# First stage of a transformer block: a sine product kept in PSUM, normalising split over two engines, loops written out, two loads moved

## The chip, the cores and the metric

One Trainium2 chip, one of its cores. The metric is the time of one execution on the device in microseconds. Engines: TensorE (PE; its weight loads are PEld), VectorE (DVE), ScalarE (ACT), GpSimd (POOL) and SyncE (SP), which only issues DMAs here. All times below are microseconds unless marked ns.

## The reference, cut to what matters

Four sequences of 1024 rows with 128 features, float32. The change is in the first part: normalise the rows, project them to queries, keys and a 32-wide latent, rotate, and apply gelu.

```python
def _layernorm(x, axis=-1, eps=1e-05):
    m = jnp.mean(x, axis=axis, keepdims=True)
    v = jnp.var(x, axis=axis, keepdims=True)
    return (x - m) / jnp.sqrt(v + eps)

def _apply_rope(x, cos, sin):
    x1, x2 = (x[..., :d // 2], x[..., d // 2:])
    return x * cos + jnp.concatenate([-x2, x1], axis=-1) * sin

# attention on xn = _layernorm(x); 16 heads of 8; E - DR = 0, so q and k are the rotated parts alone
q_r = _apply_rope(x @ wqr + bqr, cos, sin)
k_r = _apply_rope(x @ wkr + bkr, cos, sin)
ckv = _gelu(x @ wkv + bkv)
v = (ckv @ wv + bv).reshape(b, s, H, HD).transpose(0, 2, 1, 3)
q, k = _gelu(q_r), _gelu(k_r)            # split in heads
attn = softmax(causal(q k^T / sqrt(8)))  # then attn @ v, @ wo + bo, layernorm, residual
```

Behind it come a mixture of eight experts with a shared one and a last normalisation. They are as before.

## The kernel before

The kernel has one first stage, closed by a barrier of all engines, and then a long part in which attention, routing and experts overlap. The first stage cuts the 4096 rows into 8 chunks of 512 (`CHUNKS`), two to a sequence; `pair(j)` handles chunks 2j and 2j + 1, and p is the parity of a chunk. The four pairs run through `peeled`: pair 0 and pair 3 are written out, pairs 1 and 2 are a loop on each engine, with waits and addresses worked out in registers.

For chunk c the engines do this, each in its own order:

- ScalarE issues the load of x for chunk c + 2 (L501), makes the latent `ckvT` (L504), rounds the second bfloat16 part of chunk c - 1 (`part_mid`, L493, twice), copies the turned rows of chunk c + 1 from PSUM (`keep_xT`, L485), waits until the stores of chunk c - 2 have landed, and applies gelu to q and then to k, each twice: `full` in float32 (L515) and `parts` in bfloat16 (L516). Between the two it copies v (L519).
- VectorE makes four products, projection plus bias times cosine or sine (L558): q with cosine, q with sine, k with cosine, k with sine. The cosine product goes to `direct`, the sine product to `turned`, both in SBUF; a sum of both (L562) follows each sine product. After the q half come the statistics of chunk c + 2 (L325, L329, and the variance step L332), after the k half the normalising of chunk c + 2 in four tiles (L536).
- TensorE multiplies for the latent (L596), q with plain and swapped columns, then turns the normalised rows of chunk c + 1 (L583, four transposes), then k with plain and swapped columns (L599), then v (L605). The four products for VectorE lie in banks 1 to 4 of PSUM.
- GpSimd computes the inverse root for chunk c + 2 (L443), the remainder `rest` after the first bfloat16 part (L448) and the third part (`part_low`, L453), for q and for k. Its order is k's rest and both low parts of chunk c - 1, the root, then q's rest of chunk c.
- SyncE stores v and six parts of q and k of chunk c - 1 to DRAM (`store`, L396 and L400). Before the stores of chunk 5 it issues `load_group` for group 0 and before those of chunk 6 for group 1. A group is four heads of one sequence, ten DMAs (L285 to L295). Groups 0 and 1 belong to sequence 0, so chunks 0 and 1 are all that they need.

After chunk 7 TensorE waits for all products and for group 0, and computes scores for 18 items (L305); VectorE takes their row maxima (L316). The barrier follows when SyncE has seen all stores land (L421).

What orders work around the change: `pe.wait_ge(xn_ok, c + 1)` ahead of the turn; `wait(act, stored[p], ...)` ahead of the gelus of chunk c, for chunk c - 2; `wait(dve, gelu_ok, 4 * c - 4)` ahead of the products of chunk c, as `direct` has two buffers; and in PE `wait(pe, rope, ...)`, by which a bank is overwritten only after VectorE's product has read it.

## Time and profile before

| | us |
|---|---|
| median of 3 runs | 838.52 (838.01 to 841.66) |
| profiled execution | 839.22 |
| its span | 837.5 |
| TensorE busy | 753.9 (90%) |
| VectorE busy | 620.7 (74%) |
| ScalarE busy | 510.1 (61%) |
| GpSimd busy | 338.3 (40%) |
| first stage, to the barrier | 96 |

Busy is time in which an engine worked on the program's instructions, summed over the whole span; it hides that stages have different limits. For the change one reads the first 96 us alone: the busy time per stretch, and then the order of instructions on each engine with the idle time in front of each and what ended it ("<-"). A trailing q (SPq, ACTq) marks what an engine's sequencer does, here the issue of DMAs.

### The profile page before, as it was taken

How to read it: one execution, taken by the hardware profiler on the slowest of the kernel's cores; microseconds unless marked ns; L12 is line 12 of the kernel's file. 1: busy time of each engine (PE TensorE's matmuls, PEld its weight loads, DVE VectorE, ACT ScalarE, POOL GpSimd, SP SyncE). 2: the span in 40 equal slices, each digit the busy share in tenths (PEclk: the TensorE clock that was granted, in tenths of full speed). 3: DMA queues.
4: the chain of work that ended last, by engine and by line, in shares of the span. 5: the costliest groups of instructions: out<-in, count | busy, mean ns of one | idle time of the engine just before them, and what ended most of it. 6: DMA issues, size and time to landing. Idle time of an engine off the chain costs nothing.

```text
span 837.5 us, 17519 instructions
## 1 busy us (share of the span) xinstructions
PE 753.9 (90%) x5660; PEld 361.6 (43%) x5660; DVE 620.7 (74%) x1942; ACT 510.1 (61%) x1047; POOL 338.3 (40%) x517
## 2 busy tenths in 40 slices
PE   5876689999999999999999999999989889898994
PEld 2332133333334334334333433433336768786861
DVE  5998878988887896886897887888445566465636
ACT  2664046666766877766778666687887534343525
POOL 3775121222221331234543215453257276464624
PEclk9997579999999999999999999999999999999998
DMA  6459462431632423405324224141312325232153
GB/s 161 149 156 178 119 166 31 67 52 17 116 57 44 79 46 73 80 8 110 59 61 94 53 39 86 40 98 40 118 37 71 104 79 146 72 85 71 50 205 112
DMA packets 78187, 71.84 MB, mean 86 GB/s; under 512 B 26939, under 2 KB 58076, under 8 KB 77916
## 3 DMA queue, kind: packets, MB, share of 16 engines
q1 hardware_dynamic: 69472, 59.87, 32.4%
q0 software_dynamic: 4352, 8.99, 3.4%
q10 hardware_dynamic: 4274, 1.87, 0.9%
q8 instruction: 47, 0.77, 0.4%
q14 instruction: 42, 0.34, 0.1%
HBM read 44.27 MB, written 23.94 MB: 81 GB/s over the span
## 4 chain that ended last, share of the span: by engine, by line
PE 62%; DVE 11%; issue 7%; ACT 6%; POOL 1%; DMA 1%; POOLq 0%; SPq 0%; DVEq 0%; ACTq 0%
PE ps L2171 14%; PE ps L2198 14%; PE ps L305 11%; DVE x_in L316 5%; PE ps L1668 4%; ACT expT L1895 4%; PE ps L1649 2%; PE ps L1651 2%; PE ps L1657 2%; PE ps L1650 2%; PE ps L1573 1%; PE ps L2148 1%; PE ps L1586 1%; ACT rows L747 1%; PE ps L972 1%
## 5 line engine op out<-in xcount | busy, mean ns | idle before, releaser
L1895 ACT ACTIVATE expT<-ps 128x512 f32<-128x512 f32 (+1 forms) x640 | 333.0, 554 | 149.6 <-PE ps L2198 143.4
L316 DVE CUSTOM_DVE_ANT_0 x_in<-ps,mask 128x1024 bf16<-128x1024 f32 (+7 forms) x512 | 364.3, 754 | 60.5 <-PE ps L305 57.0
L2198 PE MATMUL ps<-q_space,k_space 96*128 96x512 bf16 (+3 forms) x768 | 223.6, 334 | 8.8 <-ACT expT L1895 5.1
L305 PE MATMUL ps<-k_space,q_space 96*128 96x512 bf16 (+3 forms) x768 | 197.6, 343 | 22.1 <-DVE mx L316 15.5
L2171 PE MATMUL ps<-expT,vr 128*9 128x256 f32 (+1 forms) x2560 | 178.3, 360 | 0.9 <-POOL expT L1849 0.9
L1849 POOL TENSOR_SCALAR_AFFINE_SELECT expT<-expT 128x512 f32<-128x512 f32 x128 | 79.7, 634 | 195.9 <-ACT expT L1895 195.5
L2198 PEld LDWEIGHTS ps<-q_space,k_space 96*128 96x128 bf16 x768 | 62.1, 98 | 160.3 <-ACT expT L1895 103.1
L305 PEld LDWEIGHTS ps<-k_space,q_space 96*128 96x128 bf16 x768 | 64.1, 100 | 86.2 <-DVE mx L316 49.0
L1255 POOL DMA_INDIRECT expert_rows<-expT,tile_to x72 | 69.2, 961 | 49.8 <-ACT expT L1326 24.1
L737 POOL DMA_INDIRECT sorted_rows<-rows,places x64 | 64.2, 1003 | 58.2 <-ACT expT L1895 33.9
L2171 PEld LDWEIGHTS ps<-expT,vr 128*9 128x9 f32 x2560 | 41.3, 88 | 92.2 <-issue 47.1
L1318 ACT ACTIVATE q_space<-ps 128x512 f32<-128x512 f32 x36 | 21.5, 597 | 56.4 <-PE ps L1651 56.4
L1802 POOL TENSOR_SCALAR negs<-mx 128x16 bf16<-128x16 f32 x32 | 8.4, 263 | 108.6 <-DVE mx L316 96.6
L1496 DVE TENSOR_TENSOR q_space<-q_space,ps 128x512 f32<-128x512 f32 x36 | 24.7, 687 | 35.3 <-ACT q_space L1318 35.3
L1668 PE MATMUL ps<-w_gu,k_space 128*128 x288 | 41.4, 287 | 2.5 <-DVE k_space L1503 2.4
L316 DVE DVE_READ_ACCUMULATOR2_ANT mx<- 128x1 f32 x512 | 42.5, 83 | 0.0
L1649 PE MATMUL ps<-w_hi,rows_hi 128*128 x72 | 35.4, 492 | 4.3 <-issue 2.8
L1668 PEld LDWEIGHTS ps<-w_gu,k_space 128*128 128x128 f32 x288 | 34.9, 191 | 9.8 <-issue 9.7
L1503 DVE COPY k_space<-ps 128x512 f32<-128x512 f32 x36 | 24.9, 692 | 15.5 <-PE ps L1657 15.3
L1326 ACT ACTIVATE expT<-ps,expT 128x128 f32<-128x128 f32 x72 | 22.5, 365 | 17.8 <-PE ps L1668 17.8
L1651 PE MATMUL ps<-w_hi,rows_lo 128*128 x72 | 29.5, 410 | 0.0
L1650 PE MATMUL ps<-w_lo,rows_hi 128*128 x72 | 29.4, 408 | 0.0
(228 smaller groups left out, 934.1 us busy)
## 6 DMA issues: line engine op xcount, KB each, us to landing
q_space<-q_parts SPq DMA_DIRECT2D x48, 192.0 KB
expT<-sorted_rows SPq DMA_DIRECT2D x72, 65.0 KB, 2.1
k_space<-k_parts SPq DMA_DIRECT2D x32, 128.0 KB
expT<-expert_rows SPq DMA_DIRECT2D x16, 256.0 KB, 5.4
q_parts<-parts SPq DMA_DIRECT2D x24, 128.0 KB, 2.4
k_parts<-parts SPq DMA_DIRECT2D x24, 128.0 KB, 3.2
k_space<-k_parts SPq DMA_DIRECT2D x16, 192.0 KB
v_ones<-v_st SPq DMA_DIRECT2D x8, 288.0 KB, 3.2
```

The source lines that it names most:

```text
L305: last = nc.tensor.matmul(psw[:, at + lo:at + hi], qr[:, g % RING, hh, qi * P:(qi + 1) * P], kr[:, g % RING, hh, lo:hi], start=True, stop= ...
L316: last = nc.vector.tensor_tensor_reduce(out=unread[:, odd, col:col + width], in0=psw[:, 2 * CT * odd + col:2 * CT * odd + col + width], in ...
L737: nc.gpsimd.indirect_dma_start(out=xs_d, out_offset=bass.IndirectOffsetOnAxis(ap=pos[:, q, k, c * NT + t:c * NT + t + 1], axis=0), in_=xs[ ...
L1255: nc.gpsimd.indirect_dma_start(out=y_d, out_offset=bass.IndirectOffsetOnAxis(ap=to[:, r, i:i + 1], axis=0), in_=yt[:, r, i], in_offset=Non ...
L1649: nc.tensor.matmul(out, hi, wide_hi[:, bass.ds(at, 2 * INTER)], start=True, stop=False)
L1650: nc.tensor.matmul(out, hi, wide_lo[:, bass.ds(at, 2 * INTER)], start=False, stop=False)
L1651: nc.tensor.matmul(out, lo, wide_hi[:, bass.ds(at, 2 * INTER)], start=False, stop=True).then_inc(gu_ok, 1)
L1668: last = nc.tensor.matmul(out, hT[:, q % 2, INTER * i + P * f:INTER * i + P * (f + 1)], wide_down[:, bass.ds(at + P * f, P)], start=f == 0 ...
L1849: nc.gpsimd.affine_select(out=tile, in_=tile, compare_op=ALU.is_ge, fill=0.0, base=0, pattern=[[0, GH], [1, P]], channel_multiplier=-1).th ...
L1895: act.activation(expT[:, (NS * g + s) % PTN, hh, 0:width], ps[:, B_S + hh % 2, 0:width], ACT.Exp, scale=SCALE).then_inc(exp_ok, 1)
L2171: last = nc.tensor.matmul(ps[32 * hh:32 * hh + VW, B_O + half, at:at + n], vr[:, g % RING, kt, hh * VW:(hh + 1) * VW], expT[:, (NS * g + s ...
L2198: last = nc.tensor.matmul(ps[:, B_S + hh % 2, col:col + m], kr[:, g % RING, hh, kt * P:(kt + 1) * P], qr[:, g % RING, hh, q0:q0 + m], star ...
```

## The change

It is in the first stage only. Five things change:

- The sine product is written back to the PSUM bank from which it was read, and the sum reads it there. `turned` is gone. TensorE's next product into that bank waits for the sum (`added`) instead of the product (`rope`).
- Of the four tiles of a chunk VectorE normalises two; ScalarE normalises the other two, with scale `rstd1` and bias `nb1`, a new 128 x 4 product of minus mean and inverse root that VectorE makes first. ScalarE does this at the end of its chunk, for chunk c + 2, and in the prologue for chunks 0 and 1.
- The turn on TensorE and the root on GpSimd wait for ScalarE's half too.
- The loops over pairs are written out on all engines; waits and addresses are constants.
- `load_group` for group 0 comes ahead of the stores of chunk 3 and for group 1 ahead of those of chunk 5.

```diff
@@ helpers: peeled, at_row and wait_apart are removed @@
-def peeled(eng, n, body):
-
-    body(0)
-    with eng.Fori(1, n - 1) as i:
-        body(i)
-    body(n - 1)
@@ ln_stats @@
-            wait_apart(dve, steps, base + 1, passed_dve)
+            dve.wait_ge(steps, base + 1)
@@ first stage, tiles and semaphores @@
-            turned = sb(one, "turned", [P, 2, CT])
+            nb1 = sb(one, "nb1", [P, 2, NT])
...
+            xn_act = sem(one, "xn_act")
+            nb_ok = sem(one, "nb_ok")
+            BY_DVE = NT // 2
...
+            GROUP0_AT = 4
@@ sync @@
-                    qb, kb, vb = at_row(qd, j), at_row(kd, j), at_row(vd, j)
+                    qb, kb, vb = qd[j], kd[j], vd[j]
...
-                        if not exists(j + 1, PAIRS):
-
-                            if p == 0:
-                                sp.wait_ge(rows_in, DMA * 2 * RING)
-                                for i in range(2):
-                                    sp.wait_ge(stored[i], DMA * NSTORE)
-                            load_group(sp, p)
-                        if isinstance(j, int) and j == 0:
+                        if 2 * j + p == GROUP0_AT:
+                            sp.wait_ge(rows_in, DMA * 2 * RING)
+                            for i in range(2):
+                                sp.wait_ge(stored[i], DMA * NSTORE)
+                        if 2 * j + p in (GROUP0_AT, GROUP0_AT + 2):
+                            load_group(sp, (2 * j + p - GROUP0_AT) // 2)
+                        if j == 0:
...
-                peeled(sp, PAIRS, pair)
+                for j in range(PAIRS):
+                    pair(j)
@@ gpsimd @@
                 def root(c, p):
                     pool.wait_ge(ln, 3 * c + 3)
                     wait(pool, xn_ok, c - 1)
+                    wait(pool, xn_act, c - 1)
@@ scalar @@
+                def normalize_act(c, p):
+                    act.wait_ge(nb_ok, c + 1)
+                    for t in range(BY_DVE, NT):
+                        last = act.activation(x1[:, p, t], x1[:, p, t], ACT.Identity, scale=rstd1[:, p, t:t + 1],
+                                              bias=nb1[:, p, t:t + 1])
+                    last.then_inc(xn_act, 1)
+
+                normalize_act(0, 0)
                 keep_xT(0, 0)
+                normalize_act(1, 1)
                 act.wait_ge(w_in, DMA * W_DMAS)
...
-                            act.dma_start(x1[:, p], at_row(x_v, j + 1)[p]).then_inc(x_ok[p], DMA)
+                            act.dma_start(x1[:, p], x_v[j + 1, p]).then_inc(x_ok[p], DMA)
...
+                        if exists(c + 2, CHUNKS):
+                            normalize_act(c + 2, p)
@@ vector @@
                 def normalize(c, p):
                     dve.wait_ge(rstd_ok, c + 1)
-                    for t in range(NT):
+                    nc.vector.scalar_tensor_tensor(nb1[:, p], mv1[:, p, :, 0], -1.0, rstd1[:, p], ALU.mult,
+                                                   ALU.mult).then_inc(nb_ok, 1)
+                    for t in range(BY_DVE):
...
-                            dst, table = ((direct[:, p, i // 2], cos), (turned[:, i // 2], sin))[i % 2]
-                            if i % 2:
-                                wait(dve, added, 2 * c + i // 2 - 1)
+                            dst, table = ((direct[:, p, i // 2], cos), (ps[:, 1 + i], sin))[i % 2]
...
                                 nc.vector.tensor_tensor(direct[:, p, i // 2], direct[:, p, i // 2],
-                                                        turned[:, i // 2], ALU.add).then_inc(added, 1)
+                                                        ps[:, 1 + i], ALU.add).then_inc(added, 1)
@@ tensor @@
                 def turn(c, p):
                     pe.wait_ge(xn_ok, c + 1)
+                    pe.wait_ge(xn_act, c + 1)
...
                         for i, w in enumerate((w_q, w_qs, w_k, w_ks)):
-                            wait(pe, rope, 4 * (c - 1) + 1 + i)
+                            if i % 2:
+                                wait(pe, added, 2 * (c - 1) + i // 2 + 1)
+                            else:
+                                wait(pe, rope, 4 * (c - 1) + 1 + i)
...
-                pe.wait_ge(rope, 4 * CHUNKS)
+                pe.wait_ge(added, 2 * CHUNKS)
```

## Rows read from the trace of the kernel before

**Rows 1.** The page's head: the span of the profiled execution.

```profile
span 837.5 us, 17519 instructions
```

**Rows 2.** Busy time of each engine by stretch; then granted clock, DMA share, GB/s.

```profile
16.00:58.00 42.00, 34.92 (x125) 15.95 (x124) 39.23 (x106) 26.16 (x47) 29.50 (x25) 1.00 0.51 154
...
76.00:96.00 20.00, 13.83 (x36) 2.66 (x35) 17.06 (x48) 3.82 (x7) 4.53 (x4) 0.50 0.85 192
```

**Rows 3.** Timeline (start, duration, engine, line, tiles), end of the stage; SyncE's wait there.

```profile
91.51 0.60 SPq L400 DMA_DIRECT2D k_parts<-parts  x1
95.76 0.08 DVE L316 DVE_READ_ACCUMULATOR2_ANT mx<- 128x1 f32 x1
96.13 1.28 ACT L1895 ACT_TABLE_LOAD   x1 [13.28 <-PEq L334]
...
SPq L421 <- DMA k_parts<-parts: 2.7, 1, 2.7
```

**Rows 4.** Timeline of VectorE: one chunk, and the variance step of another.

```profile
34.18 0.74 DVE L558 SCALAR_TENSOR_TENSOR direct<-ps,cols,cos 128x512 f32<-128x512 f32 x1
...
35.62 1.50 DVE L562 TENSOR_TENSOR direct<-direct,turned 128x512 f32<-128x512 f32 x1
37.03 1.10 DVE L536 TENSOR_SCALAR x_in<-x_in,mv,rstd 128x128 f32<-128x128 f32 x4
...
40.74 0.87 DVE L325 BATCH_NORM_STATS2 st<-x_in 128x6 f32<-128x128 f32 x4 [0.56 <-DMA x_in<-in_x]
...
42.28 0.75 DVE L558 SCALAR_TENSOR_TENSOR direct<-ps,cols,cos 128x512 f32<-128x512 f32 x1
...
57.80 0.72 DVE L332 TENSOR_SCALAR ve<-mv 128x4 f32<-128x4 f32 x1
```

**Rows 5.** Timeline of GpSimd: one rest, and two low parts.

```profile
35.41 1.15 POOL L448 TENSOR_TENSOR rest<-full,parts 128x512 f32<-128x512 f32 x1
...
55.75 2.74 POOL L453 TENSOR_TENSOR parts<-rest,parts 128x512 bf16<-128x512 f32 x2
```

**Rows 6.** Timeline of ScalarE behind the k sum of one chunk.

```profile
37.14 0.63 ACT L515 ACTIVATE full<-direct 128x512 f32<-128x512 f32 x1 [2.25 <-DVE direct L562]
...
38.77 0.61 ACT L493 ACTIVATE parts<-rest 128x512 bf16<-128x512 f32 x1
```

**Rows 7.** Operations like the new ones, elsewhere: ns min/median/max; for ScalarE busy, mean ns.

```profile
L1496 DVE TENSOR_TENSOR q_space<-q_space,ps x36: 686/686/689, 675.4 to 794.3; 128x512 f32<-128x512 f32 x36
...
L1907 DVE MEMSET ps<- x1: 912/912/912, 96.4 to 96.4; 128x1024 f32 x1
...
L1370 DVE SCALAR_TENSOR_TENSOR out_shift<-out_mean_var,out_rstd x8: 146/146/164, 813.8 to 830.7; 128x4 f32<-128x4 f32 x8
...
L747 ACT ACTIVATE attn_rows<-attn_rows,shift,rstd 128x128 f32<-128x128 f32 x28 | 13.7, 495 | 0.2 <-DVE shift L823 0.2
```

**Rows 8.** The load of x: an issue in the timeline, and us to landing of all six.

```profile
37.61 0.39 ACTq L501 DMA_DIRECT2D x_in<-in_x  x1
...
DMA to landing us min/median/max: 2.8/3.0/4.5
```

**Rows 9.** Timeline: group 0's first DMA; ScalarE's q gelu of chunks 5 and 7.

```profile
62.88 0.36 SPq L285 DMA_DIRECT2D q_space<-q_parts  x1
...
57.55 0.63 ACT L515 ACTIVATE full<-direct 128x512 f32<-128x512 f32 x1 [0.61 <-DMA k_parts<-parts]
...
78.28 0.63 ACT L515 ACTIVATE full<-direct 128x512 f32<-128x512 f32 x1 [6.82 <-DMA k_parts<-parts]
```

**Rows 10.** Timeline of TensorE: turn of chunk 7, its last product, the first scores.

```profile
62.36 0.66 PE L583 MATMUL ps<-identf,x_in 128*128 128x128 f32 x4 [1.64 <-DVE x_in L536]
...
69.41 1.02 PE L599 MATMUL ps<-xnT,w_ks 128*128 128x512 f32 x2
...
75.93 1.55 PE L305 MATMUL ps<-k_space,q_space 96*128 96x512 bf16 x4 [4.41 <-DMA q_space<-in_const]
```

**Rows 11.** TensorE by stretch: length, busy (instructions), granted clock, DMA share, GB/s.

```profile
70.63:74.05 3.42, 0.89 (x8) 1.00 1.04 155
...
671.38:674.79 3.41, 3.01 (x9) 0.50 0.24 86
```

## What the change is predicted to do, and why

> **What bounds the kernel now.** I read the windows by stage first, then the end of the first stage, then one chunk of it engine by engine. The execution took 839.22 us, 1.7 over its span of 837.5 [rows 1]; the median of the three timed runs is 838.52, 0.7 below it. The change touches only the first stage, which ends at a barrier: VectorE ends its 18th maximum at 95.84, SyncE sees its last store landed at 91.51 + 0.60 + 2.7 = 94.8, and the next stage starts at 96.1 [rows 3]. So two paths end together there, 1.0 us apart. In the steady part VectorE is busy 39.23 of 42.00 us, GpSimd 29.50, and the DMA engines have a mean share of 0.51 [rows 2].
>
> One chunk of 512 rows takes 8.1 us, from its third product at 34.18 to the next one's at 42.28 [rows 4]. VectorE inside it: the k sum at 35.62 which takes 1.50, four normalisings of 1.10, and later a wait of 0.56 for x before the statistics [rows 4]. The 1.50 is a hold: GpSimd's rest runs 35.41 to 36.56, and the sum ends 0.55 after it; against a PSUM operand the same shape takes 0.69 and always does (686/686/689) [rows 4, 5, 7]. The variance step shows the same hold: at 57.80 it takes 0.72 and ends at 58.52, just behind GpSimd's two low parts, 55.75 to 58.49 [rows 4, 5]. So a second path of about the same length runs k sum, ScalarE, GpSimd's low parts, variance step.
>
> **Part by part.** Let s be the start of the third product of a chunk (34.18).
> - *Sine product in PSUM.* The k sum ends at s + 1.44 + 0.69 = s + 2.13, not s + 2.94. The write into PSUM is not in the trace for this operation. The nearest row, a memset of 1024 columns into PSUM, took 0.91, 0.46 for 512 [rows 7], so the write doesn't limit a product of 0.74; I take 0.74. The bounds are 0.60 and 0.90, 0.3 us a chunk either way.
> - *The hold moves on.* The new shift (0.15 by its twin in the last stage, [rows 7]) has two SBUF inputs, and it now arrives at s + 2.1 while GpSimd's rest still runs, to s + 2.38 [rows 5]. So the shift waits 0.3 and ends at s + 2.5; two normalisings of 0.26 pitch end at s + 3.0. Before it was s + 3.87. VectorE gains 0.85 a chunk. Unheld it would be 1.1, held by the whole rest again 0.5.
>   The Trainium skill (SBUF — State Buffer, section Who interferes with whom) says that an instruction with at most one SBUF input doesn't contend with GpSimd, and that two SBUF inputs or a two-port tensor_scalar do. By its rule the sum is freed, but the shift and the normalising behind it stay exposed, which speaks against part of the gain: 0.85, where the freed sum and two normalisings less would give 1.1. The trace agrees [rows 4, 5, 7].
> - *Half the normalising on ScalarE.* Two of 0.49, with an overlap of 0.06 each, are 0.86 [rows 7]. They stand behind both gelus of the k half and ahead of everything else of ScalarE. The queue behind the k sum runs full, parts, ckvT in 1.63 (37.14 to 38.77), then mid in 0.61 [rows 6]; GpSimd's first low part needs that mid. It now starts at the sum + 1.66 + 0.86 + 0.61 + 0.16 = sum + 3.3. The low parts took 2.74, with a hold by VectorE's q sum in it; two like the rest of 1.15 are 2.3 [rows 5], and the q sum's operand is in PSUM now, so I take 2.3. They end at s + 2.13 + 3.3 + 2.3 = s + 7.7, and hold the variance step until then. So the chunk falls from 8.1 to 7.7, not to the 7.15 that VectorE alone would take. TensorE's turn of the next rows waits for ScalarE's half, at the sum + 2.0, not only for VectorE's. Over the three chunks before the load that is 0.4 each, less 0.5 that I allow for the prologue, where ScalarE still issues the weights' DMAs and loads a table: 0.7 in all. TensorE's products wait for the sum instead of the product in alternate banks; these are done 3 us ahead, cost 0.
> - *Loops written out.* The x load of the next chunk but one was issued at 37.61, 0.49 after the k sum, and lands after 3.0 (2.8/3.0/4.5) [rows 4, 8]. It now stands behind the shift's wait, at s + 2.6, lands at s + 5.6 and is wanted at s + 5.1. This 0.5 is inside the 7.7. The bounds are 0 and, if ScalarE issued it only when its second normalising starts, 1.0 later: a chunk of 8.0.
> - *Rows of groups 0 and 1.* SyncE issued group 0's ten DMAs from 62.88, ahead of the stores of chunk 5. They filled the ring: those stores landed for ScalarE at 78.28, 15.4 us after the load's start, and ScalarE stood still for 6.82; without a load it waits 0.61 in the same place [rows 9]. Now the load stands ahead of the stores of chunk 3. It starts two chunks of 8.1 earlier, at 46.7 in the old time, 45.4 in the new (0.7 by the shorter chunks, 0.6 of loop work on SyncE between its issues). So chunk 3's stores land at 45.4 + 15.4 = 60.8, and 1.0 later with one load of x beside them. I take 61.8; the bounds are 58 (the DMA engines idle half the time) and 64. ScalarE needs them for the first gelu of chunk 5, which it was ready for at 57.55 - 0.61 = 56.9 and would now be at 55.6. It stands still for 6.2.
>   Queued behind this wait on ScalarE are that gelu, parts, v and the two k gelus, 0.54 each (three in 1.63), and then its half of normalising chunk 7: 5 x 0.54 + 0.86 = 3.6. So TensorE's turn of chunk 7 comes at 61.8 + 3.6 = 65.4. Before, it came at 62.36 [rows 10], after VectorE alone. TensorE is in order: the k products of chunk 6, v, and all of chunk 7 stand behind the turn, 8.1 us to the end of the last product (62.36 to 70.43) [rows 10]. TensorE would be through at 73.5. But it will have been idle some 5 us, from about 60. After it ran 0.89 us in the 3.42 before 74.05 its granted clock was 0.50, the lower level [rows 11]; so I expect the lower level when it resumes, and full clock back after dense work, as at 671.38 to 674.8 [rows 11]. That costs half of the dense time at the lower level, some 5.3 us: 2.7. TensorE is through at 76.2, VectorE's last product and sum end 1.5 later, at 77.7.
>   Before, VectorE ended at 74.0, but the scores started at 75.93, when group 0 had landed after a wait of 4.41 [rows 10]. So this wait of 1.9 goes and the scores start 1.8 later, at 77.7.
> - *18 maxima.* 19.9 us from scores to the end at the lower clock. I take 0.4 off, for the first 3.4 us at full clock; the bounds are 0 and 2 (full clock throughout). The stage ends at 77.7 + 19.9 - 0.4 = 97.2, 1.4 later than 95.84.
> - *Stores.* Group 1's load stands where group 0's stood, so chunk 5's stores land near 78 again and ScalarE goes on as before to 84.4. The stores of chunk 7 no longer stand behind a second load: they end near 91.5, not 94.8. This path no longer sets the end.
>
> The sum: 839.22 + 1.4 = 840.6; 0.7 less for the median is 839.9. I round to **839.7 us**.
>
> **The rivals.**
> 1. *The load is hidden* (faster). In the steady part the DMA engines have half their time free [rows 2]. If the ring drains by 56, ScalarE never stands still, TensorE's turn comes 1.3 before the old 62.36, at 61.1 (the sum 2.2 earlier by five shorter chunks and its own 0.8, ScalarE's half 0.9 later than VectorE's four were), its end at 69.2, VectorE's at 70.7; the maxima end at 90.2. Then the stores decide, at 89 (group 1's load 2 us earlier) to 91.5. The stage is 4.3 to 5.8 shorter: 833 to 834. For it: the free half. Against: the 15.4 us are from the same pattern of issues, load and then stores, on the same ring. Chance 0.22.
> 2. *TensorE stays at the lower clock* (slower). Place: the 8.1 us behind the turn of chunk 7. If the clock doesn't come back during it, it takes 16.2 in place of 10.8; end of stage 102.6, total 845. It decides if the clock is still at 0.50 when chunk 7's first product runs. For it: between 76 and 96 TensorE worked 13.83 of 20 us and stayed at 0.50 [rows 2]. Against: the recovery at 674.8 [rows 11]. Chance 0.10.
> 3. *ScalarE issues x late.* Chunks of 8.0, so load and stall come 1 us later, 841. The trace shows x issued at 37.61 behind a gelu of 37.14 and its twin, so with one activation in front of it not yet started, and no deeper case [rows 6, 8]. Chance 0.10. The Trainium skill (Advanced Engine Details and Errata, section Engine Queue Depths) gives ScalarE a queue of 8; by it x would be issued as soon as the shift is made, and this rival would not occur.
> 4. *The normalising doesn't go cheaply to ScalarE.* If Identity and Gelu needed different tables, two table loads of 1.28 [rows 3] would come in each chunk: 10.3 in place of 8.1, over six chunks 13 more, 852. Between exponentials it needed none (28 of 495 ns) [rows 7]. Chance 0.03.
>
> **How the numbers follow.** The forecast has 0.55, and its own range, from a load landing at 58 to 64 with the clock kept or lost, is 836.5 to 843. A difference of 0.5% (4.2 us) is about what a measurement of this kernel tells from none. Faster by more: 0.20, most of rival 1. Slower by more: 0.15, rivals 2 and 4 and the forecast's upper tail. Within: 0.65. The range for 8 in 10 takes in rival 1 and leaves out rivals 2 and 4 and a little more: 833.0 to 844.0.
>
> **What would show it.** The sum with PSUM at 0.69 in every chunk; the shift held to 0.4; chunks of 7.7; ScalarE's first gelu of chunk 5 idle for 4 to 7 us on a store; TensorE idle before the turn of chunk 7, with the clock at 0.50 behind it; scores within 0.3 of VectorE's last sum; the stage's end at 95 to 98. If ScalarE doesn't stand still there, rival 1 holds and the stage ends near 91.

## Result, and the profile after

| | before | after |
|---|---|---|
| median, us (5 runs each) | 838.52 (837.08 to 841.66) | 845.19 (843.81 to 848.76) |
| ratio to before | | 1.0077, 95% interval 1.0043 to 1.0111 |
| profiled execution, us; its span | 839.22; 837.5 | 848.76; 847.0 |
| end of the first stage (table load of the next one) | 96.13 | 105.90 |
| third product of chunks 0, 1, 2 and 5 | 18.21, 26.20, 34.18, 58.44 | 23.69, 31.14, 39.05, 66.53 |

The kernel became slower by 6.7 us, under 1%, where 1.2 was forecast. In the profiled execution the whole loss lies in the first stage: its end comes 9.8 us later, the span is 9.5 longer. That execution is the longest of its five, 3.6 above their median; a long stretch at TensorE's lower clock, shown below, has about that size.

The first stretch of it, timelines of SyncE, ScalarE's queue and VectorE in the changed kernel (start, duration, engine, line, operation, tiles; in brackets how long the engine stood still, and what released it):

```profile
9.63 0.38 SPq L268 DMA_DIRECT2D k_space<-in_const  x1
...
11.39 0.30 SPq L268 DMA_DIRECT2D q_space<-in_const  x1
...
11.83 0.40 ACTq L489 DMA_DIRECT2D x_in<-in_x  x1
...
22.29 0.87 DVE L298 BATCH_NORM_STATS2 st<-x_in 128x6 f32<-128x128 f32 x4 [5.53 <-DMA x_in<-in_x]
...
23.69 0.74 DVE L549 SCALAR_TENSOR_TENSOR direct<-ps,cols,cos 128x512 f32<-128x512 f32 x1
```

The rows of chunk 2 are asked for at 11.83. ScalarE's order now has its half of normalising chunk 1 ahead of this load, and that half waits for VectorE's shift; so the load also comes behind all six constant fills of SyncE. VectorE has chunk 2's rows at 22.29, after 10.5 us. Before the change the same load was issued beside the first fill, and VectorE found the rows in place (timelines of the kernel before):

```profile
9.74 0.42 ACTq L501 DMA_DIRECT2D x_in<-in_x  x1
...
16.82 0.86 DVE L325 BATCH_NORM_STATS2 st<-x_in 128x6 f32<-128x128 f32 x4
```

Chunk 0's third product is 5.5 us late. Only the shorter chunks eat into that: 4.9 at chunk 2, 3.6 at chunk 4 (53.97 for 50.38).

One undisturbed chunk, VectorE, GpSimd and ScalarE's queue, to compare with [rows 4 to 6]:

```profile
46.51 0.74 DVE L549 SCALAR_TENSOR_TENSOR direct<-ps,cols,cos 128x512 f32<-128x512 f32 x1
47.17 0.74 DVE L549 SCALAR_TENSOR_TENSOR ps<-ps,cols,sin 128x512 f32<-128x512 f32 x1
47.95 0.69 DVE L553 TENSOR_TENSOR direct<-direct,ps 128x512 f32<-128x512 f32 x1
48.55 0.27 DVE L526 SCALAR_TENSOR_TENSOR nb<-mv,rstd 128x4 f32<-128x4 f32 x1
...
52.02 0.87 DVE L298 BATCH_NORM_STATS2 st<-x_in 128x6 f32<-128x128 f32 x4 [0.63 <-DMA x_in<-in_x]
...
53.34 0.71 DVE L305 TENSOR_SCALAR ve<-mv 128x4 f32<-128x4 f32 x1
53.97 0.74 DVE L549 SCALAR_TENSOR_TENSOR direct<-ps,cols,cos 128x512 f32<-128x512 f32 x1
...
51.76 2.27 POOL L431 TENSOR_TENSOR parts<-rest,parts 128x512 bf16<-128x512 f32 x2 [0.70 <-ACT parts L481]
...
48.87 0.37 ACTq L489 DMA_DIRECT2D x_in<-in_x  x1
```

The sum takes 0.69, the write into PSUM costs nothing (0.74), the shift 0.27. The low parts start at 51.76, held by ScalarE's mid copy, and end at 54.03; the variance step, 0.71 where 0.17 is its own time, ends with them. The chunk takes 7.46, from 46.51 to 53.97.

Around the load of group 0, SyncE, ScalarE, VectorE and TensorE:

```profile
50.47 0.49 SPq L258 DMA_DIRECT2D q_space<-q_parts  x1
...
56.33 0.37 ACTq L489 DMA_DIRECT2D x_in<-in_x  x1
...
66.92 0.63 ACT L503 ACTIVATE full<-direct 128x512 f32<-128x512 f32 x1 [6.79 <-DMA k_parts<-parts]
...
65.13 0.87 DVE L298 BATCH_NORM_STATS2 st<-x_in 128x6 f32<-128x128 f32 x4 [6.29 <-DMA x_in<-in_x]
...
69.76 0.86 ACT L469 ACTIVATE x_in<-x_in,nb,rstd 128x128 f32<-128x128 f32 x2
...
70.72 1.09 PE L576 MATMUL ps<-identf,x_in 128*128 128x128 f32 x4 [6.25 <-DVE x_in L529]
```

Two engines stand still for two different transfers. ScalarE waits 6.79 for chunk 3's stores. VectorE waits 6.29 for chunk 7's rows, which ScalarE's queue asked for at 56.33 and which took 8.8 us instead of the 3.0 of [rows 8]. Both waits end within 2 us of each other, and the turn of chunk 7 comes at 70.72, for 62.36 in [rows 10]. The bracket names VectorE, whose two tiles are done at 69.83; ScalarE's two end at 70.62, and the turn follows them. ScalarE's wait of [rows 9], 6.82 at chunk 7's first gelu, was as long, but nothing that TensorE needed stood behind it.

TensorE behind that turn by stretch (length, busy time of PE, PEld, DVE, ACT and POOL with instructions, granted clock, DMA share, GB/s), and then, as a timeline, the end of the stage:

```profile
71.00:75.00 4.00, 4.00 (x8) 1.61 (x6) 1.60 (x3) 2.74 (x6) 3.30 (x4) 0.50 1.05 156
...
79.00:83.00 4.00, 4.00 (x6) 1.85 (x6) 0.93 (x2) 1.72 (x3) 3.39 (x3) 0.50 0.57 206
```

```profile
86.41 0.82 PE L278 MATMUL ps<-k_space,q_space 96*128 96x512 bf16 x3 [0.64 <-DVE direct L553]
...
105.53 0.09 DVE L289 DVE_READ_ACCUMULATOR2_ANT mx<- 128x1 f32 x1
105.90 1.28 ACT L1892 ACT_TABLE_LOAD   x1 [16.47 <-PEq L307]
```

TensorE was busy the whole time from 71 to 83 and stayed at 0.50, the 1.2 GHz level. The scores start at 86.41, when the last sum is done and not, as in [rows 10], when rows land; the 18 maxima end 19.2 us later, and the next stage's table load stands at 105.90 for the 96.13 of [rows 3].

### The profile page after: what moved, and what is told of

Read it like the earlier page. It is cut to its first block, busy times and chain, and to the rows that moved or that the text cites. A ratio compares the mean times of both kernels' runs of the same rounds, so it can differ in the third digit from the quotient of the medians.

```text
span 847.0 us, 17322 instructions
## 1 busy us (share of the span) xinstructions
PE 758.4 (90%) x5660; PEld 363.7 (43%) x5660; DVE 611.1 (72%) x1934; ACT 515.8 (61%) x1063; POOL 335.3 (40%) x517
## 4 chain that ended last, share of the span: by engine, by line
PE 61%; DVE 10%; issue 7%; ACT 6%; POOL 2%; DMA 1%; POOLq 0%; SPq 0%; DVEq 0%; ACTq 0%
PE ps L2168 14%; PE ps L2195 14%; PE ps L278 11%; DVE x_in L289 5%; PE ps L1665 4%; ACT expT L1892 4%; PE ps L1646 2%; PE ps L1654 2%; PE ps L1648 2%; PE ps L1647 2%; PE ps L2145 1%; ACT rows L744 1%; PE ps L1583 1%; PE ps L1570 1%; PE ps L969 1%
```

## Experiments

Every ratio is to the kernel before, run on the same chip. The chips differ: from the last group of attention products (`ps<-expT,vr`) to the end it took 205.5 us in the profile of before and 205.9 in that of the changed kernel, 205.8 to 207.2 in those of another chip, and 218.2 to 225.8 in those of three more, with any kernel. So the stage's end is read from each trace (before: 96.13, one execution), and the ratio beside it. What a ratio is worth in us is its distance from 1 times the median of before on that chip.

**Chunk 2's rows first** (x_first).

```
 keep_xT(0, 0)
+act.wait_ge(xT_ready, 1)
+act.dma_start(x1[:, 0], x_v[1, 0]).then_inc(x_ok[0], DMA)
 normalize_act(1, 1)
...
-if exists(j + 1, PAIRS):
+if exists(j + 1, PAIRS) and c > 0:
```

> The changed kernel, with one edit: ScalarE issues the load of chunk 2's rows right behind its first copy of turned rows, ahead of its half of normalising chunk 1 and so ahead of SyncE's six constant fills (9.63 to 11.39 us). In the changed kernel this load was issued at 11.83 and landed at 22.29, before the change 9.74 and 14.22; the third product of chunk 0 came at 23.69 instead of 18.21. Theory A (the load stood behind the fills on the DMA engines, and what it delayed is never made up): rows land by 15, the third product of chunk 0 is near 18.5, every later event of the stage 5.2 us earlier, stage end near 100.4, median near 840.0. The wait of ScalarE for chunk 3's stores (6.79) stays, near 62 instead of 67. Rival B (the delay is taken up by the later waits for the group load and for the clock): third product earlier, but the stage end moves by under 1.5 us, median 844 to 845. Rival C (the late landing comes from the new order of other loads, not from the fills): rows land after 20 again, no change of time.

Ratio 1.0042 (1.0022 to 1.0062). ScalarE's queue, VectorE and TensorE:

```profile
10.01 0.40 ACTq L476 DMA_DIRECT2D x_in<-in_x  x1
...
17.48 0.87 DVE L298 BATCH_NORM_STATS2 st<-x_in 128x6 f32<-128x128 f32 x4
...
61.37 0.63 ACT L505 ACTIVATE full<-direct 128x512 f32<-128x512 f32 x1 [6.50 <-DMA k_parts<-parts]
...
60.06 0.87 DVE L298 BATCH_NORM_STATS2 st<-x_in 128x6 f32<-128x128 f32 x4 [6.47 <-DMA x_in<-in_x]
...
65.64 1.08 PE L578 MATMUL ps<-identf,x_in 128*128 128x128 f32 x4 [6.43 <-issue]
```

VectorE doesn't wait for chunk 2's rows any more, and its third product comes at 18.88, the turn of chunk 7 at 65.6 instead of 70.7: the 5 us are kept up to there. The stage ends at 97.26, 3 us before theory A's 100.4; that rest is the clock (below): from the turn to the first scores it took 12.1, not 15.7. The ratio is worth 3.6 us, where theory A's median is 1.5 above that of before.

**The changed kernel again** (after_again), no edit.

> The changed kernel as it is, a second look, on the same chip as the three kernels beside it. In its first profile TensorE stood at a granted clock of 0.50 for 13.65 us behind the turn of chunk 7 (69.31 to 82.96), and that execution was the longest of its five. With the rows of chunk 2 loaded first, the stretch at 0.50 was some 6.5 us (63.6 to 70) behind the same idle time. Theory A (the length of the stretch varies from execution to execution, by up to 3.5 us of time): the late start repeats (third product of chunk 0 at 23.7, turn of chunk 7 near 70.7), and the third product of chunk 7 comes either 10.0 us behind the turn, stage end near 102.4, or 13.5 behind, 105.9. Theory B (the stretch of 13.65 belongs to this kernel): 105.9 again. The ratio to the kernel before, 1.0077 on the first chip, between 1.005 and 1.012 in both.

Ratio 1.0120 (1.0098 to 1.0142), stage end 102.37. Windows of the same form as above:

```profile
71.00:75.00 4.00, 3.93 (x9) 2.02 (x9) 1.49 (x3) 3.10 (x6) 3.29 (x4) 0.59 1.01 123
75.00:79.00 4.00, 4.00 (x15) 2.07 (x16) 2.21 (x4) 2.72 (x6) 1.71 (x3) 1.00 1.05 196
```

The late start repeats (VectorE has chunk 2's rows at 22.51), and so does the turn, at 71.1; the higher level is back by 75, not by 83. Theory A holds: the long stretch is not this kernel's in every execution. This profiled execution is the shortest of its six, as the first was the longest of its five. The ratio on this chip is no better than the first, so one profile says little of the median here.

**Loads at their old places** (loads_back), and with the first edit too (x_first_loads_back).

```
-GROUP0_AT = 4
+GROUP0_AT = 6
+GROUP1_AT = 7
...
```

> The changed kernel, with the loads of groups 0 and 1 put back ahead of the stores of chunks 5 and 6, as before the change. Everything else of the change stays, the late start too. Theory A (the load at chunk 4 costs a wait of 6.8 us of ScalarE and a lower clock behind it, 8.0 us from 69.3 on): period of 7.45 kept from 23.69, third product of chunk 7 at 75.8, VectorE's last sum 78, group 0's rows land at 65.4 + 12.9 = 78.3, scores at 78.4, stage end near 98, 7.6 us less than 105.6: median 838 to 841. ScalarE's wait for stores moves to the first gelu of chunk 7 and costs nothing there. Rival B (the chunks' time, not the load's place, sets the stage: the load would collide with the same thing wherever it stands): ScalarE waits as long and TensorE's turn of chunk 7 is as late, median 844 to 846.

> Both edits of the two kernels before: chunk 2's rows are loaded ahead of the constant fills, and the group loads stand where they stood before the change. What is left of the change is the product kept in PSUM, half of the normalising on ScalarE and the written-out loops. Theory A (these three parts make a chunk shorter, 7.45 for 8.1 us, and the two others took it away and more): third product of chunk 0 at 18.4, of chunk 7 at 70.6, VectorE's last sum 72.7, group 0's rows land at 60.1 + 12.9 = 73.0, 18 maxima 19.9, stage end 93.0 against 95.8: median 835 to 836.5. Rival B (the shorter chunks gain nothing, because the end is set by the stores or by the landing of group 0, which stay where they were): 838 to 839. The gains of the two edits add up if A holds: 845.2 less 5.2 less 4 to 7.

Loads back: stage end 98.24, as theory A had it, ratio 1.0051 (1.0033 to 1.0069), above its median. Both: stage end 92.93, ratio 0.9987 (0.9973 to 1.0001). From 102.37, the second profile of the changed kernel, the first edit alone takes 5.1, the second 4.1, both 9.4: there the two losses add. From 105.90 it is 8.6, 7.7 and 13.0, less than their sum, as each edit alone already takes away the long stretch at the lower clock. In the last kernel the scores wait 4.02 for group 0's rows and start at 72.74, as theory A had it (73.0). The ratio is worth 1.1 us only, where the stage ended 3.2 earlier than in the profile of before; it lies between theory A and rival B.

**Fills behind chunk 2's load** (fills_wait): the changed kernel, SyncE waits before the fills.

```
 if j == 0:
+    sp.wait_ge(xn_act, 2)
```

> The changed kernel; SyncE holds the six constant fills until ScalarE has normalised its half of chunk 1, so that they are issued at about the time of the load of chunk 2's rows (11.8 to 12.1) and not 2.2 us ahead of it. The load itself is issued as late as in the changed kernel. Theory A (it landed after 10.4 us because it stood behind the fills): it lands after 3 to 5 us, by 17, third product of chunk 0 at 20.5 instead of 23.7 to 23.9, stage end 3 us earlier. Rival B (not the fills, but the lateness of the issue, or another load): lands after 20 again.

```profile
12.28 0.41 ACTq L490 DMA_DIRECT2D x_in<-in_x  x1
13.15 0.38 SPq L268 DMA_DIRECT2D k_space<-in_const  x1
...
16.68 0.86 DVE L298 BATCH_NORM_STATS2 st<-x_in 128x6 f32<-128x128 f32 x4
...
26.88 0.87 DVE L298 BATCH_NORM_STATS2 st<-x_in 128x6 f32<-128x128 f32 x4 [3.92 <-DMA x_in<-in_x]
```

The load is as late as in the changed kernel, but ahead of the fills, and VectorE finds its rows in place at 16.68: it was the fills. But now the next load of x, issued at 20.44, is waited for until 26.88: the fills, issued from 13.15 to 15.2, are the likely reason, not shown by an edit of their own. The turn of chunk 7 came at 66.9, the low clock was long again (0.50 in every window from 67 to 79), stage end 102.09, ratio 1.0086 (1.0063 to 1.0110). That is 3.8 earlier than in the first profile of the changed kernel, but only 0.3 than in the second, whose clock came back sooner, and the ratio is no better.

**Only the loops written out** (unrolled), **with the new places of the loads** (unrolled_loads), both from the kernel before, with its SBUF sums and four normalisings on VectorE.

> The kernel before the change, with only the loops of the first stage written out; products, normalising and loads as they were. Theory A (the loops cost only SyncE and the register work between issues, some 0.6 us of a load's start): median 838 to 838.5, within 0.1% of the kernel before. Rival B (longer code is fetched beside the stage's own DMAs, and the time lost in the changed kernel's first stage is partly this): 840 or more, with idle time of every engine at the same moments.

> The kernel before, loops written out, and the group loads at the places of the change (ahead of the stores of chunks 3 and 5), nothing else: all four normalisings on VectorE, both sums from SBUF. TensorE's turn of chunk 7 waits here for nothing of ScalarE. Theory A (the harm of the load goes through ScalarE's half of normalising alone, as I predicted): ScalarE stands still 4.7 us to 62.6, but the turn of chunk 7 comes at 63 as with the loads at their old places, third product of chunk 7 at 72, scores at 74.7 instead of 75.3, stage end 94. Theory B (the load also starves the load of chunk 7's rows on ScalarE's own ring, which took 9.0 us, 51.07 to 60.04, in the kernel with only chunk 2's rows first): x issued at 53.8 lands at 62.7, VectorE waits for it 5 us, turn at 68, third product of chunk 7 at 77 to 79, scores near 80, stage end 98 to 99.5, some 4 us over the kernel with its loops written out only (1.0025 of before): ratio 1.006 to 1.008.

Loops alone: stage end 95.11, 1.0 earlier; ratio 1.0025 (1.0005 to 1.0045), above theory A's 0.1%. Its chunks take 8.24 (42.63 to 50.87), VectorE working without a gap, unlike rival B's picture. So in this trace the loops cost the stage nothing, and why the whole was not faster stays open. With the loads moved: stage end 101.82, 6.7 more, ratio 1.0049 (1.0032 to 1.0067).

```profile
62.08 0.87 DVE L325 BATCH_NORM_STATS2 st<-x_in 128x6 f32<-128x128 f32 x4 [3.90 <-DMA x_in<-in_x]
...
62.95 0.63 ACT L516 ACTIVATE full<-direct 128x512 f32<-128x512 f32 x1 [5.28 <-DMA k_parts<-parts]
...
67.40 1.11 PE L586 MATMUL ps<-identf,x_in 128*128 128x128 f32 x4 [5.87 <-DVE x_in L538]
```

Here the turn needs nothing of ScalarE, and it is still late, 67.40 for 63.0. My path through ScalarE is not the only one: chunk 7's rows, asked for at 54.14, 7.5 us behind the load's start, take 7.9 us. Theory B's mechanism holds in the trace; the stage ends 2.3 behind its range, and the ratio is 0.1% below it.

**Which of the two holds the turn?** Three kernels, all with chunk 2's rows first: VectorE normalises all of chunk 7 (x_first_dve7); the group load waits until ScalarE has issued chunk 7's rows (behind_x7); both (behind_x7_dve7).

```
-    for t in range(BY_DVE):
+    for t in range(NT if c == CHUNKS - 1 else BY_DVE):
...
-if exists(c + 2, CHUNKS):
+if exists(c + 3, CHUNKS):
     normalize_act(c + 2, p)
...
-pe.wait_ge(xn_act, c + 1)
+pe.wait_ge(xn_act, min(c + 1, CHUNKS - 1))
```

```
 if 2 * j + p == GROUP0_AT:
+    sp.wait_ge(xn_act, 7)
```

> The changed kernel with chunk 2's rows loaded ahead of the constant fills (its turn of chunk 7 came at 65.6: ScalarE's wait for stores ended at 61.4, VectorE's wait for chunk 7's rows at 60.1), and VectorE normalises all four tiles of chunk 7, so that the turn waits for nothing of ScalarE. Theory A (both things hold the turn, each by about as much): turn at 64.6 to 65.0, VectorE having waited for the rows to 60. Theory B (ScalarE's standing still alone made it late, as I forecast): turn at 60 to 61, third product of chunk 7 near 69.

> The changed kernel with chunk 2's rows loaded ahead of the fills, and the load of group 0 held by SyncE until ScalarE has normalised its half of chunk 6, at 52.8, behind the issue of chunk 7's rows at 51.1 and 7.6 us later than otherwise; chunk 3's stores go behind it as before. Theory A: chunk 7's rows land within 3.5 us, VectorE's third product of chunk 5 on time at 56.2 instead of 61.5; ScalarE waits for chunk 3's stores to 52.8 + 16.4 = 69.2, and the turn of chunk 7, with ScalarE's half queued behind that, comes 3.7 later, at 72.9: the wait of ScalarE is enough by itself. Theory B (ScalarE's wait does no harm by itself): turn before 64.

> Both edits of the two kernels before: the group load behind the issue of chunk 7's rows, and chunk 7 normalised by VectorE alone. Theory A: nothing of the group load reaches the turn of chunk 7 now; it comes at 60 to 61, though ScalarE still waits for chunk 3's stores to 69; VectorE's products of chunk 7 wait for the gelus of chunk 5 instead, to 69.2 + 2.9 = 72, so the third product of chunk 7 comes at 73.5. Theory B (turn after 64): a third path that I have not named.

Timelines of TensorE and ScalarE, of x_first_dve7:

```profile
65.20 1.12 PE L578 MATMUL ps<-identf,x_in 128*128 128x128 f32 x4 [6.62 <-DVE x_in L531]
```

of behind_x7:

```profile
66.98 0.63 ACT L506 ACTIVATE full<-direct 128x512 f32<-128x512 f32 x1 [12.75 <-DMA k_parts<-parts]
...
70.52 1.08 PE L579 MATMUL ps<-identf,x_in 128*128 128x128 f32 x4 [11.96 <-issue]
```

and of behind_x7_dve7:

```profile
67.46 0.63 ACT L506 ACTIVATE full<-direct 128x512 f32<-128x512 f32 x1 [12.99 <-DMA k_parts<-parts]
...
59.04 0.66 PE L579 MATMUL ps<-identf,x_in 128*128 128x128 f32 x4 [0.23 <-DVE x_in L532]
...
70.75 2.07 PE L604 MATMUL ps<-w_v,ckvT 33*128 33x128 f32 x8 [9.33 <-ACT ckvT L495]
```

Taking ScalarE out of the path moves the turn from 65.6 to 65.2. Leaving only ScalarE in it, the turn comes 3.5 behind the end of its wait, at 70.5 (the load started at 52.2 and the stores landed 14.8 us behind it, not 16.4, and so both are some 2.3 earlier than expected). With neither it is on time, 59.0. Theory A holds in all three: each is enough by itself. The third shows one more path, which I had missed: the v product of chunk 6 waits 9.33 for a gelu queued behind the same wait of ScalarE, so the third product of chunk 7 came at 79.4, not 73.5. The times were 854.19, 857.59 and 856.03, one execution each, against a median of 852.57 of before.

**The clock** (ballast): the changed kernel, TensorE kept busy before the turn of chunk 7. The products are written to a bank that is not read.

```
+if i == 1 and c in (6,):
+    for _ in range(7):
+        nc.tensor.matmul(ps[:, 7], w[:], xnT[:, p], start=True, stop=True)
 if i == 1 and exists(c + 1, CHUNKS):
     turn(c + 1, 1 - p)
```

> The changed kernel with seven more products of 512 columns on TensorE (0.85 us each at the higher clock) into a bank that nobody reads, in chunk 6 ahead of the turn of chunk 7, where it stood idle 5.8 to 6.25 us, waiting for ScalarE. They change no result and end before the turn could start. Theory A (the idle time lowers the clock, and the low clock then costs 1.5 to 5 us of the stage): granted clock 1.00 from the turn on, at 71, to the end of the last product, which comes 8.1 us behind it instead of 9.3 to 14; scores at 80.5 instead of 82.6 (second look) or 86.4 (first), stage end 100 or less, ratio 1.002 to 1.006 below the changed kernel's. Rival B (the clock falls from something else, at a fixed time or by the DMA traffic beside it): 0.50 from 69 on as before, and no gain, or the seven products delay the turn.

TensorE's timeline, and the windows:

```profile
65.31 6.17 PE L598 MATMUL ps<-xnT,w_qs 128*128 128x512 f32 x14
72.95 0.63 PE L576 MATMUL ps<-identf,x_in 128*128 128x128 f32 x4 [1.47 <-issue]
```

```profile
65.00:73.00 8.00, 6.54 (x17) 2.63 (x16) 5.50 (x18) 3.70 (x8) 2.98 (x3) 1.00 0.95 250
...
77.00:81.00 4.00, 4.00 (x10) 1.52 (x9) 2.41 (x4) 2.76 (x6) 3.27 (x4) 1.00 0.98 249
```

With TensorE busy the granted clock stayed at 1.00, and the third product of chunk 7 came 7.8 us behind the turn, against 9.3 and 13.5 in the two profiles of the changed kernel. The idle time does lower the clock. No gain is seen here: chunk 7's rows took 10.0 us this time (57.33 to 67.36), the turn came at 73, scores at 82.9 (80.5 expected), stage end 102.70, ratio 1.0103 (1.0079 to 1.0127), between the two of the changed kernel. Theory A was right on the clock, wrong on the stage's end.

**The product in PSUM alone** (unrolled_psum, with the wait for `added` on TensorE as in the change), from the kernel before with its loops written out, and **ScalarE's half in another order** (mid_first), from x_first_loads_back.

```
-((direct[:, p, i // 2], cos), (turned[:, i // 2], sin))[i % 2]
+((direct[:, p, i // 2], cos), (ps[:, 1 + i], sin))[i % 2]
...
```

```
-part_mid(c - 1, 1 - p, 0)
 part_mid(c - 1, 1 - p, 1)
...
+part_mid(c, p, 0)
 if exists(c + 2, CHUNKS):
     normalize_act(c + 2, p)
...
```

> The kernel before, loops written out, and the sine product kept in PSUM, nothing else: four normalisings on VectorE, loads at their old places. Theory A (VectorE's gain of 0.8 to 1.0 us in each of the two sums is kept, as there is no half on ScalarE that holds back its mid copies): a chunk falls from 8.24 us to 7.0 to 7.3, and the stage ends 3 us earlier at 92, the loads starting as much earlier: ratio 0.996 to 0.998, and half of the normalising on ScalarE brings nothing. Theory B (the hold moves to the first of the normalisings, two-port operations that run into GpSimd's rest, and the variance step is held behind the low parts): a chunk of 7.5 to 7.9, stage end 93.5: ratio 0.998 to 1.000.

> The kernel with chunk 2's rows loaded ahead of the constant fills and the group loads at their old places (product in PSUM, half of the normalising on ScalarE), where a chunk takes 7.46 us. One edit: ScalarE makes the mid copy of the q half ahead of its half of the normalising, not behind it. With the product in PSUM and all four normalisings on VectorE a chunk takes 6.85: so this half, meant as relief, costs 0.6. Theory A (it holds back the mid copies, then GpSimd's low parts, and these hold the variance step, 0.64 for 0.17): the low parts start at once, the variance step takes 0.17, a chunk 6.9 to 7.0, the rest being the wait for x, which is issued behind the shift. Stage end 93 less 6 x 0.5 = 90, ratio to the kernel before 0.995. Rival B (the wait for x alone sets the chunk): variance step at 0.17, the wait for x grows by the same 0.5, a chunk of 7.4, ratio 0.998 to 1.000.

GpSimd's low parts and VectorE's variance step behind them, in the kernel with ScalarE's half ahead of both mid copies (x_first_loads_back):

```profile
45.75 2.27 POOL L432 TENSOR_TENSOR parts<-rest,parts 128x512 bf16<-128x512 f32 x2 [0.70 <-ACT parts L484]
...
47.44 0.60 DVE L305 TENSOR_SCALAR ve<-mv 128x4 f32<-128x4 f32 x1
```

with the product in PSUM alone (unrolled_psum):

```profile
43.58 2.28 POOL L454 TENSOR_TENSOR parts<-rest,parts 128x512 bf16<-128x512 f32 x2
...
45.89 0.17 DVE L332 TENSOR_SCALAR ve<-mv 128x4 f32<-128x4 f32 x1
```

and with one mid copy first (mid_first):

```profile
43.47 2.42 POOL L432 TENSOR_TENSOR parts<-rest,parts 128x512 bf16<-128x512 f32 x2
...
45.75 0.17 DVE L305 TENSOR_SCALAR ve<-mv 128x4 f32<-128x4 f32 x1
```

PSUM alone gives a chunk of 6.82 us (32.33 to 52.79 for three), stage end 89.47 and ratio 0.9950 (0.9932 to 0.9968), better than either theory. ScalarE's half of the normalising, added to it, makes a chunk 0.6 longer. With the one mid copy first it costs nothing and gains nothing: chunks of 6.87 and 6.98, stage end 89.79, ratio 0.9951 (0.9934 to 0.9968).

**Loads that do less harm.** Group 0 one chunk later and group 1 behind all stores, with chunk 2's rows first (load5_last); group 0's ten DMAs in three pieces, on unrolled_psum (psum_spread); the same pieces on mid_first (mid_first_spread).

```
-GROUP0_AT = 4
+GROUP0_AT = 5
...
-if 2 * j + p in (GROUP0_AT, GROUP0_AT + 2):
-    load_group(sp, (2 * j + p - GROUP0_AT) // 2)
+if 2 * j + p == GROUP0_AT:
+    load_group(sp, 0)
...
 store(PAIRS - 1, 1)
+load_group(sp, 1)
```

```
+if 2 * j + p in (4, 5, 6):
+    load_piece(sp, 2 * j + p - 4)
```

`load_piece` issues 3, 4 and 3 of the ten DMAs; group 1's stand behind the last store here too.

> The changed kernel with chunk 2's rows loaded ahead of the constant fills, group 0's rows loaded ahead of the stores of chunk 4 (one chunk later than in the changed kernel, one earlier than before it), and group 1's behind all stores of the stage. Theory A (a group load does harm only through what is issued behind it and is wanted soon: a load of x, and the stores that the next gelus but one wait for; all loads of x are issued by 51, and nothing that VectorE or TensorE does waits for the gelus of chunk 6): load at 52.6, ScalarE waits in the first gelu of chunk 6 until 69 and nobody behind it waits, group 0's rows in by 66, VectorE's last sum at 70.2 as without a load, scores at 70.3, stage end 90.2 at the lower clock or 88.5 at the higher, 3 to 4 us less than the 92.9 of the kernel with the loads at chunks 5 and 6. Ratio to the kernel before 0.994 to 0.996. Rival B (the load delays chunk 7's x or sums wherever it stands in the middle): scores after 75, ratio above 1. Rival C (the stores become the end, because ScalarE's wait of 8 us moves the last gelus to 80): last stores land at 92 or later, ratio 0.999.

> The kernel before with loops written out and the sine product in PSUM (stage end 89.5, where TensorE waits 4.1 us for group 0's rows until 69.3, VectorE's last sum ending at 66.6), and the ten DMAs of group 0 spread over three chunks: three ahead of chunk 3's stores, four ahead of chunk 4's, three ahead of chunk 5's; group 1's all behind the last store. Theory A (in pieces of 3 to 4 us the load fits beside rows and stores, as the DMA engines are idle half the time there): x is waited for by under 1 us, scores at 67 to 68.5, stage end 87 to 88.5, ratio 0.991 to 0.994. Rival B (any piece ahead of stores delays the gelus two chunks later as much as it takes itself, and these the sums): the chunks grow to 8 in the middle, scores after 69.3, ratio 0.995 or more, as without the spreading.

> What gained, in one kernel: product in PSUM, half of the normalising on ScalarE with the mid copy of the q half ahead of it, chunk 2's rows ahead of the fills, group 0's DMAs spread over three chunks and group 1's behind the last store. With the loads at their old places and no spreading the stage ended at 89.8 (ratio 0.9951), with the spreading but all normalising on VectorE at 87.1 (0.9942). Theory A (the gains add: scores no longer wait for group 0's rows): scores at 68 to 69, stage end 87.5 to 88.5, ratio 0.992 to 0.994. Rival B (ScalarE's half stands behind its waits for stores, which each piece of the load makes longer, so turns come late): scores after 70, ratio 0.995 to 0.998.

The first: stage end 91.49, ratio 0.9975 (0.9958 to 0.9992), between theory A and rival C. VectorE was through at 69.4 (70.2 expected), but the scores began at 71.68, not 70.3, because TensorE's v product stood before them:

```profile
70.60 1.16 PE L604 MATMUL ps<-w_v,ckvT 33*128 33x128 f32 x8 [3.04 <-ACT ckvT L495]
71.68 1.15 PE L278 MATMUL ps<-k_space,q_space 96*128 96x512 bf16 x4
```

It waits for the gelu of ckvT, queued behind ScalarE's wait for stores (5.81, until 67.31). The second did what theory A said: scores at 67.34 behind VectorE's last sum, stage end 87.14, ratio 0.9942 (0.9922 to 0.9962), at the edge of its range. The third: VectorE waited 2.20 for chunk 7's rows, scores at 72.41, stage end 92.20, as rival B had it; its ratio was still 0.9936 (0.9913 to 0.9958), as theory A had it. These two intervals and that of unrolled_psum overlap. What is shown is a gain of about 0.5% (some 4 us) for a kernel with the product in PSUM, loops written out, and no half on ScalarE (with the half, mid_first comes to the same); that the spreading adds to it is seen in the trace alone.

## Why the prediction was wrong

- *Sum in PSUM, write, shift*: right. 0.69, 0.74, and 0.27 where 0.15 + 0.3 of hold was taken; only once, right behind chunk 7's late rows, the shift took 0.74. From SBUF, with the loops written out, the sums took 1.41 and 1.70. The Trainium skill (SBUF — State Buffer, section Who interferes with whom) says that a VectorE instruction contends with GpSimd if it has two SBUF inputs or runs in a two-port mode, and not if it has at most one SBUF input. The traces agree: the sum is freed, the variance step still held, 0.71 in the chunk shown and 0.60 to 0.74 in x_first_loads_back beside the low parts, and 0.17 behind them.
- *ScalarE's half holds the mid copies*: right. The chunk took 7.46, forecast 7.7; mid_first and unrolled_psum show that this order costs 0.6 of the 1.4 that the freed sums bring (8.24 to 6.82). I had read the second path in the profile, and it was this that made the half worthless.
- *Prologue*: this step failed, and it is the largest. I counted the late issue of x, behind the shift's wait, in the steady chunk, and put 0.5 down for the whole prologue. In the prologue it is ScalarE's half for chunk 1 that stands ahead of chunk 2's load and moves it past SyncE's six fills. It cost 5.5 us at the third product of chunk 0; x_first brings this product to 18.88, and fills_wait shows that it is the fills.
- *Load 0 and the stores behind it*: right in size, shifted by the prologue. Start 50.47 (forecast 45.4), stores landed 16.4 us later (15.4 + 1.0), ScalarE stood still for 6.79 (6.2), the turn followed 3.8 behind (3.6).
- *What the load does to x*: not in the sum. Chunk 7's rows are asked for on ScalarE's queue, 6 us behind the load's start, and took 8.8 us, 8.4 to 10.0 in the other traces of this order. It changes the turn little here, since ScalarE's path is as long. In the kernel before, where the turn needs nothing of ScalarE, it is the path by which the load makes the turn late (unrolled_loads: 67.40 for 63.05, with 6.7 more of stage). Rival 1, the hidden load, is refuted: with half the DMA time free on average, a load of that size in one piece is not hidden; in three pieces it nearly was in one kernel (psum_spread, VectorE waited 0.40 for chunk 7's rows), not in the other (2.20).
- *Clock*: the mechanism was right and the size open. I forecast 5.3 us at the lower level, which no row gave, and 2.7 of loss. Behind the turn it was 12.2 us in the first profile (70.72 to some 82.96) and 3.3 in the second (0.59 in the window from 71 to 75). From turn to first scores the two took 15.7 and 11.5, forecast 12.3. So the first profile met the condition of rival 2 (0.50 when chunk 7's first product ran), with 14.0 us from the turn to the last product's end where 16.2 was its price; the second did not.
- *Maxima and stores*: right. 19.2 us (19.5), and SyncE saw the last stores land at 96.5, off the path.
- Rival 3 didn't occur: x was issued at s + 2.36, with the shift's end. Nor did rival 4: no table load stands between ScalarE's gelus and its normalising.

The sum of it, for the first profile: the last maximum forecast at 97.2, measured at 105.6, 8.4 later; 5.1 of them are there when the load starts, 0.2 more at the turn, 3.4 between turn and scores, with the clock, and the maxima give 0.3 back. In the second profile the turn is 5.7 late, and turn to scores gives 0.8 back; its table load stands at 102.37, 3.5 before the first's. The median was 5.5 above the forecast, the size of the prologue, but that the prologue explains it alone isn't shown: without this loss (x_first) the ratio is still worth 3.6 us, where the forecast is 1.2.

One agreement is luck. The median, 845.2, equals rival 2's total of 845, but only the first profile shows the long stretch at the lower clock; in the second the stage ended 6.2 later than in the kernel before, without that stretch. A slip besides: the sum of the prediction gives 839.9, which it calls rounded to 839.7; no term stands behind this 0.2.

What stays open: in eleven of the thirteen experiments with a ratio, the ratio is worth 1.4 to 4.0 us more than the stage ends give against the one profile of before (loops alone: stage 1.0 shorter, time 2.1 longer, interval 0.4 to 3.8), in two 1.5 less (unrolled_loads, mid_first_spread). In the first profile of the changed kernel it is 3.3 less. The 96.13 of before may be a late one among its executions, as the changed kernel's 105.90 was; there is no second profile of before.

## What to carry to other kernels

When an edit moves a DMA's issue behind a new wait, look at it in the first iteration too: what another queue puts in front there may cost far more than in the steady state (here 5.5 us, where 0.5 was taken). A large load harms not only what is queued behind it on its own ring, but small loads of other engines issued after it; place it behind the last of them, or cut it into pieces that fit between them (that was enough in one trace of two). And before work is moved to a less busy engine, ask what in that engine's order it pushes back: here half the normalising, put before a copy that another engine needed, gave up 0.6 of the 1.4 us per chunk that the freed sums brought.

## What the runs showed of the hardware

- A load of x, 256 KB, had landed 2.9 us after its issue with nothing ahead of it (x_first) and 3.6 beside stores (after_again). Up to VectorE's first use it took 10.3 to 10.5 behind six fills that another engine had begun to issue 2.2 us and ended 0.4 us earlier (four traces), and 7.9 to 10.0 behind a group load of ten DMAs that began 5.8 to 7.5 us earlier (seven traces).
- Stores issued right behind such a group load on the same queue had landed for ScalarE 14.8 to 17.1 us after the load's start (sixteen traces).
- After 5.8 to 6.6 us without work TensorE's granted clock stood at 0.50, and under back-to-back products it came back after very different times: the third product of chunk 7 came 9.3, 9.9, 9.9, 12.4, 13.5 and 13.5 us behind the turn in six traces with that idle time ahead, 10.0 in one with 12.0 us idle (behind_x7), and 7.8 where seven unused products had filled it. What decides between them no run shows.
